# A gated cross-attention block on one core: context columns stay in order, work moves to VectorE, and two queues load the context

## The chip, the cores and the metric

The kernel runs on one core of a Trainium2 chip. The metric is the device time of one execution in microseconds; several runs are timed and the median is taken. One further execution is recorded by the hardware profiler.

## What is computed

Eight sequences of 100 rows (width 2048) attend to 722 context vectors each, in float32; then a linear layer with unpacked 6-bit weights follows.

```python
x = x + tanh(g_xattn[0]) * xattn(layernorm(x), ctx)      # x (8,100,2048), ctx (8,722,2048)
x = x + tanh(g_ffn[0]) * ffn(layernorm(x), qweight, scale, zero, bias)
# xattn: a = q @ k^T ; e = softmax(a) ; c = e @ k         (keys are also the values)
# ffn:   w = (unpack6(qweight) - zero) * scale ; x @ w^T + bias     (2048 x 2048)
```

## The kernel before

Every engine runs a list of instructions written out by hand, and semaphores tie the lists together. There is no scheduler: an engine that waits holds up all that stands behind it in its list, and SyncE's transfers are such a list too.

**Layout.** The context of batch `b` lies in `raw[:, b % 2]`, so there are two buffers and the loads for batch b overwrite batch b-2. It has 6 tiles (`NT`) of up to 128 keys. A tile is loaded in four pieces, one for each quarter of the 2048 columns (`g`, 512 columns each), and quarter g goes to partitions 32g to 32g+31. Tiles 0 to 2 are the first half of the keys and 3 to 5 the second. For the value product the same data is cut into 12 units of up to 64 keys (`UNITS`; unit u lies in tile u/2).

**Stages.** While batches last, TensorE goes round this loop for i = 0 to 6: `scores(i + 1)` (queries times keys, with the transposes of batch i's probabilities, `probs`, in between), then `attend(i)` (probabilities times values, with the transposes of batch i+2's queries, `queries`, in between). In this text a stage of batch i starts where `attend(i)` starts, and A is that moment. VectorE takes the row maximum of the scores at the same time.

- `keys_turned` (VectorE, `rT<-raw`, line 930): 16 transposes per batch, each over 12 blocks of 32x32 for two column groups, 768 columns wide. Eight belong to the first half of the keys and eight to the second. A ring of five (`RING`) lets five of the next batch be done during `attend`. Their input is read as `(k j c)`: neighbouring elements of a block lie 16 floats apart.
- `context_hi` (ScalarE, line 583) rounds a unit to float32r into one of five slots of `vhi`; `context_lo` (GpSimd, line 526) subtracts that from the unit and writes the rest to `vlo`. TensorE needs both. A tile may be overwritten when its units' low parts are made (`lo_made`) and its keys turned (`s_keys`). The transfers of the next batch but one wait for this (`used`).
- `probs`, `probs_lo`, `copy_probs`: the transposed probabilities are split in two parts and then copied by ScalarE (line 621, ten copies of 1200 columns: `MOVES`, shifts c = 1, 2, 3) to the other partition quarters.
- `ln1_norm` (ScalarE, line 587) normalizes the next queries in `xa`, 2048 columns at once, and `queries` transposes them with a column step of 16. `ln1_stats` (VectorE, line 753) takes their statistics in four pieces between the transposes of the second half. `residual` (VectorE, line 805) adds the attention result, `ln2_norm` (ScalarE, line 597) normalizes that for the linear layer, `x1_out` and `rows_out` (SyncE, lines 352 and 357) store both.

**SyncE's list** for batch b: `next_x(b)`, `x1_out(b-3)`, `rows_out(b-4)` (waits for `ln2_norm`), tiles 0 to 2 (line 328), `next_xres`, tiles 3 to 5.

**After the loop** come `attend(7)` with its preparations (`unpack` of the weights on VectorE, lines 858 to 865, and `copy_last_probs`, line 828, 20 copies of 600 columns), and then the linear layer, line 1158.

## Time and profile before

| | us |
|---|---|
| timed runs, median of 3 (lowest to highest) | 668.67 (666.34 to 671.26) |
| the profiled execution, own time | 658.23 |
| span of the profile, first to last instruction | 656.4 |
| TensorE busy | 553.9 |
| VectorE busy | 423.8 |
| ScalarE busy | 283.0 |
| GpSimd busy | 258.6 |
| mean granted TensorE clock, share of full | 0.937 |

The sum of a prediction is made against 658.23, the profiled execution's own time, and carried over to the median by its ratio. An engine's busy time says how much it does, not whether anything waits for it; the timeline and the chain of waits say that.

### The profile page before, as it was taken

To read this page: it belongs to the slowest core of one execution; us is meant where nothing else is said; L and a number is where in the kernel's file an instruction comes from. 1 tells how busy PE (TensorE), PEld (TensorE's weight loads), DVE (VectorE), ACT (ScalarE), POOL (GpSimd) and SP (SyncE) were. 2 spreads that over 40 slices of the span, in tenths; PEclk is the share of its full clock that TensorE was granted. 3 is DMA by queue.
4 is the path that set the end of the run, shared out by engine and by line. 5 is a ranking of instruction groups with operands and counts; after the bars stand their busy time and mean duration, and the time that the engine had idled before them with its cause. 6 is when DMAs were issued, how large, how long until landed. Compare 5 with 4: busy or idle time off the path is not lost.

```text
span 656.4 us, 10122 instructions
## 1 busy us (share of the span) xinstructions
PE 553.9 (84%) x4134; PEld 320.1 (49%) x4134; DVE 423.8 (65%) x538; ACT 283.0 (43%) x308; POOL 258.6 (39%) x245
## 2 busy tenths in 40 slices
PE   5746999999986897997997683296999999999997
PEld 5523565475553463463463352165565444444445
DVE  4649747949818918928917638959476856763544
ACT  1301755776863774675674542365342322120000
POOL 2008049389396197198197056657100000000000
PEclk8769899999999999899999596689899999999999
DMA  8999729847398498498499432447784599993321
GB/s 192 208 243 222 185 74 225 215 120 216 89 220 214 129 211 214 135 228 209 139 219 209 157 116 83 182 155 226 260 275 113 154 186 186 237 221 76 84 69 36
DMA packets 58376, 113.77 MB, mean 173 GB/s; under 512 B 21967, under 2 KB 22223, under 8 KB 54047
## 3 DMA queue, kind: packets, MB, share of 16 engines
q1 hardware_dynamic: 41580, 108.13, 63.1%
q10 hardware_dynamic: 16750, 5.01, 6.7%
q8 instruction: 32, 0.52, 0.3%
q14 instruction: 14, 0.11, 0.1%
HBM read 89.26 MB, written 19.66 MB: 166 GB/s over the span
## 4 chain that ended last, share of the span: by engine, by line
PE 35%; DVE 23%; DMA 17%; POOL 12%; ACT 5%; SPq 4%; issue 4%; DVEq 0%; ACTq 0%
PE S L1158 16%; DVE rT L930 11%; POOL vlo L526 11%; DMA xa<-in_x 9%; PE pv L1158 7%; PE S L1067 5%; DMA raw<-in_ctx 5%; DMA raw<-in_L_ffn_qweight 3%; DVE stats L753 3%; SPq L328 3%; DVE ph L828 2%; PE T L1036 2%; DVE raw L858 2%; PE pv L1098 1%; DVE xres L805 1%
## 5 line engine op out<-in xcount | busy, mean ns | idle before, releaser
L930 DVE STREAM_TRANSPOSE rT<-raw 128x768 f32<-128x768 f32 x129 | 183.6, 1471 | 110.8 <-DMA raw<-in_ctx 108.1
L526 POOL TENSOR_TENSOR vlo<-raw,vhi 128x1024 fp32r<-128x1024 f32 x96 | 218.4, 2313 | 28.1 <-ACT vhi L583 28.1
L1067 PE MATMUL S<-rT,qT 128*100 128x338 f32 (+3 forms) x544 | 187.2, 491 | 48.3 <-DVE rT L930 46.8
L1067 PEld LDWEIGHTS S<-rT,qT 128*100 128x100 f32 x544 | 90.8, 182 | 134.4 <-DVE rT L930 77.0
L1098 PE MATMUL pv<-vhi,ph 32*100 32x512 f32 (+1 forms) x736 | 127.7, 402 | 9.3 <-POOL vlo L526 9.3
L1098 PE MATMUL S<-vhi,ph 32*100 32x512 f32 (+1 forms) x736 | 128.1, 402 | 0.0
L583 ACT ACTIVATE vhi<-raw 128x1024 fp32r<-128x1024 f32 x96 | 94.7, 1018 | 33.3 <-PE S L1098 29.1
L621 ACT ACTIVATE ph<-ph 32x1200 fp32r<-32x1200 f32 (+1 forms) x70 | 84.1, 1202 | 36.6 <-DVE ph L819 35.0
L1098 PEld LDWEIGHTS pv<-vhi,ph 32*100 32x100 f32 (+1 forms) x736 | 62.7, 161 | 34.0 <-POOL vlo L526 15.6
L1158 PE MATMUL S<-raw 128*128 128x512 f16 x320 | 73.8, 387 | 5.1 <-issue 5.1
L1098 PE MATMUL S<-vlo,ph 32*100 32x512 f32 (+1 forms) x368 | 74.4, 392 | 0.0
L1098 PE MATMUL pv<-vlo,ph 32*100 32x512 f32 (+1 forms) x368 | 73.8, 392 | 0.0
L506 POOL TENSOR_SCALAR ln<-mr 100x1 f32<-100x1 f32 x16 | 4.2, 261 | 176.3 <-DVE mr L761 175.8
L1098 PEld LDWEIGHTS S<-vhi,ph 32*100 32x100 f32 (+1 forms) x736 | 63.4, 161 | 5.3
L1158 PEld LDWEIGHTS S<-raw 128*128 128x128 f16 x320 | 31.4, 99 | 42.6 <-ACT raw L565 5.3
L1158 PE MATMUL pv<-raw 128*128 128x512 f16 x192 | 42.6, 379 | 0.0
L1036 PE MATMUL T<-ident,xa 100*128 100x100 f32 (+2 forms) x176 | 26.2, 296 | 15.2 <-DVE ph L819 9.5
L650 ACT ACTIVATE xa<-raw 128x2048 f16<-128x2048 f16 x8 | 15.3, 1910 | 51.9 <-DVE raw L865 46.6
L908 DVE TENSOR_TENSOR late<-S,consts 128x512 f32<-128x512 f32 (+2 forms) x19 | 12.8, 673 | 34.0 <-PE S L1158 34.0
L1036 PEld LDWEIGHTS T<-ident,xa 100*128 100x128 f32 (+2 forms) x176 | 22.9, 207 | 22.6 <-issue 16.1
L1098 PEld LDWEIGHTS pv<-vlo,ph 32*100 32x100 f32 (+1 forms) x368 | 31.5, 162 | 4.3
L565 ACT ACTIVATE qT<-T 128x400 f32<-128x400 f32 x28 | 12.9, 499 | 47.3 <-PE T L1036 47.3
(107 smaller groups left out, 577.4 us busy)
## 6 DMA issues: line engine op xcount, KB each, us to landing
raw<-in_ctx SPq DMA_DIRECT2D x160, 256.0 KB, 8.9
raw<-in_L_ffn_qweight SPq DMA_DIRECT2D x16, 768.0 KB, 8.1
rows_scratch<-xres SPq DMA_DIRECT2D x8, 800.4 KB
xres<-in_x SPq DMA_DIRECT2D x8, 800.0 KB
x_scratch<-xres SPq DMA_DIRECT2D x8, 800.0 KB
late<-x_scratch SPq DMA_DIRECT2D x24, 256.0 KB, 6.6
out_y<-late SPq DMA_DIRECT2D x23, 256.0 KB, 3.8
xa<-in_x SPq DMA_DIRECT2D x6, 800.0 KB
```

What stands on the lines that cost most here:

```text
L328: sp.dma_start(tile_at(b, t)[32 * g:32 * g + 32, 0:whole * W].rearrange("i (k e) -> i k e", k=whole), ctx_in[b, first:last, g * W:(g + 1) ...
L526: pool.tensor_tensor(vlo[:, k, 0:n], keys, vhi[:, k, 0:n].bitcast(F32), ALU.subtract).then_inc(s_vlo, 1)
L583: act.activation(vhi[:, k, 0:n], keys, ACT.Copy).then_inc(s_vhi, 1)
L621: act.activation(ph[dst:dst + n, c], ph[src:src + n, 0].bitcast(F32), ACT.Copy).then_inc(s_copied, 1)
L650: act.activation(wn[n % 2], unp[n % 2].rearrange("p j g -> p (j g)").bitcast(F16), ACT.Copy, bias=-float(BIAS16)).then_inc(s_wn, 1)
L753: dve.bn_stats(stats[0:R, k, c, :], src[0:R, c * 512:(c + 1) * 512]).then_inc(s_stat[k], 1)
L828: dve.tensor_copy(ph[dst:dst + n, c, :, tiles, :], ph[src:src + n, 0, :, tiles, :].bitcast(F32)).then_inc(s_copied_last, 1)
L930: dve.transpose(rT[:, step % RING, 0:n * blocks * 32], keys[:, c:c + n]).then_inc(s_keys, 1)
L1036: last = pe.transpose(dst(T[k]), src, ident[0:n, 0:n])
L1067: last = pe.matmul(into[0:R, g, begin:begin + width], qT[:, c + e, :], rT[:, step % RING, e * blocks * 32:e * blocks * 32 + width], start= ...
L1098: last = pe.matmul(pv[g][0:R, :], probabilities(g, block, p), v[32 * g:32 * g + r, k, h * W:(h + 1) * W], start=(block == 0 and a == 0), s ...
L1158: last = pe.matmul(ACC[(j + k) % NA][0:r, cols], xT[m][:, h, c, :], WT[nb % 2][:, c, cols], start=(c == 0 and h == 0), stop=(c == CH - 1 a ...
```

## The change

Six things are edited together.

1. The keys are read for the transposes as `(k c j)`, 32 neighbouring floats at a time. The queries are put in the same column order: `centred` writes batches 0 and 1 in that order to `xres`, and `ln1_norm` becomes four operations of 512 columns into a new buffer `xq`, each waiting until TensorE has transposed the one before it. `queries` is spread over blocks 3, 6, 9 and 12 of `attend` instead of two at 11 and two at 15.
2. `load_ctx` now has an issuing engine. SyncE issues quarters 0 and 2 and ScalarE quarters 1 and 3 of every tile. ScalarE's issues stand at fixed places in its list.
3. VectorE takes the four copies with shift c = 3 from ScalarE (after transpose 8).
4. VectorE takes `context_lo` of unit 8 from GpSimd, ahead of the next batch's five transposes.
5. SyncE issues tiles 0 and 1 ahead of `rows_out`, and `next_x` waits for the normalization, not the transposes.
6. `unpack(1)` moves behind the copies of the last batch's probabilities.

```diff
+    ON_VECTOR = {8}
...
+            xq = attention.enter_context(nc.sbuf_tensor("xq", [P, 512], F32))
...
-            eng.wait_ge(s_vlo, b * UNITS + u + 1)
+            by = int(u in ON_VECTOR)
+            same = [v for v in range(UNITS) if (v in ON_VECTOR) == (u in ON_VECTOR)]
+            eng.wait_ge(s_vlo[by], b * len(same) + same.index(u) + 1)
...
+        def load_ctx(eng, quarters, b, t):
+            if b >= 2:
+                for u in (2 * t, 2 * t + 1):
+                    lo_made(eng, b - 2, u)
+                eng.wait_ge(s_keys, BASE[b - 2] + (FIRST_HALF[b - 2] if t < HALF else len(STEPS[b - 2])))
...
+            for g in quarters:
+                eng.dma_start(tile_at(b, t)[32 * g:32 * g + 32, 0:whole * W].rearrange("i (k e) -> i k e", k=whole),
+                              ctx_in[b, first:last, g * W:(g + 1) * W].rearrange("(k i) e -> i k e", i=32)).then_inc(s_raw[b % 2][t], 16)
+            if whole < 4:
+                for g in quarters:
+                    eng.dma_start(tile_at(b, t)[32 * g:32 * g + REST, whole * W:(whole + 1) * W],
+                                  ctx_in[b, last:last + REST, g * W:(g + 1) * W]).then_inc(s_raw[b % 2][t], 16)
...
-                k, u = bank("q", b - 1, 3)
-                sp.wait_ge(s_turned[k], u + 1)
+                sp.wait_ge(s_q, b * NCH)
...
             for b in range(2, B):
                 if b >= 3:
                     next_x(b)
                     x1_out(b - 3)
-                if b >= 4:
-                    rows_out(b - 4)
                 for t in range(HALF):
-                    used(b - 2, t)
-                    load_ctx(b, t)
+                    load_ctx(sp, (0, 2), b, t)
+                    if b >= 4 and t == 1:
+                        rows_out(b - 4)
...
                     next_xres(b - 2)
                 for t in range(HALF, NT):
-                    used(b - 2, t)
-                    load_ctx(b, t)
+                    load_ctx(sp, (0, 2), b, t)
...
-            def ln1_norm(b):
+            def ln1_norm(b, f):
                 act.wait_ge(s_rstd[0], b + 1)
-                act.activation(xa[0:R, 0:D], xa[0:R, 0:D], ACT.Identity, bias=shift[0:R, 0:1], scale=mr[0:R, 0, 1:2]).then_inc(s_q, 1)
+                k, u = bank("q", b - (f == 0), (f - 1) % 4)
+                act.wait_ge(s_turned[k], u + 1)
+                columns = xa[0:R, 0:D].rearrange("r (g c j) -> r c g j", g=Q, j=32)[:, 4 * f:4 * f + 4]
+                act.activation(xq[0:R, :].rearrange("r (c g j) -> r c g j", g=Q, j=32), columns, ACT.Identity,
+                               bias=shift[0:R, 0:1], scale=mr[0:R, 0, 1:2]).then_inc(s_q, 1)
...
                 for c, dst, n, src in MOVES:
-                    act.activation(ph[dst:dst + n, c], ph[src:src + n, 0].bitcast(F32), ACT.Copy).then_inc(s_copied, 1)
+                    if c < 3:
+                        act.activation(ph[dst:dst + n, c], ph[src:src + n, 0].bitcast(F32), ACT.Copy).then_inc(s_copied[0], 1)
...
+            for t in range(NT):
+                load_ctx(act, (1, 3), 0, t)
...
             contexts_hi(0, range(SLOTS))
+            for t in range(HALF):
+                load_ctx(act, (1, 3), 1, t)
...
+            for t in range(HALF, NT):
+                load_ctx(act, (1, 3), 1, t)
...
                 exps(i + 1)
+                if i + 2 < B:
+                    ln1_norm(i + 2, 0)
+                    for t in range(2):
+                        load_ctx(act, (1, 3), i + 2, t)
                 context_hi(i, 5)
                 if i + 2 < B:
-                    ln1_norm(i + 2)
-                    contexts_hi(i, range(6, 10))
-                    queries(i + 2, (0, 1))
-                    contexts_hi(i, range(10, UNITS))
-                    queries(i + 2, (2, 3))
-                    contexts_hi(i + 1, range(SLOTS))
+                    for f, units in enumerate(((6,), (7, 8), (9,), (10, 11))):
+                        if f < 3:
+                            ln1_norm(i + 2, f + 1)
+                        queries(i + 2, (f,))
+                        contexts_hi(i, units)
+                        if f in (1, 3):
+                            load_ctx(act, (1, 3), i + 2, 2 + f // 2)
+                    for u in range(SLOTS):
+                        context_hi(i + 1, u)
+                        if u in (1, 4):
+                            load_ctx(act, (1, 3), i + 2, 4 + u // 4)
...
             def centred(b):
                 dve.wait_ge(s_aggr[0], b + 1)
-                for p in [xa[0:R, c * 512:(c + 1) * 512] for c in range(NCH)] if b == 0 else [xa[0:R, 0:D]]:
-                    dve.tensor_scalar(p, p, mr[0:R, 0, 0:1], None, ALU.subtract).then_inc(s_q, 1)
+                turned = xres[b][0:R, 0:D].rearrange("r (c g j) -> r g c j", g=Q, j=32)
+                for g in range(Q):
+                    dve.tensor_scalar(turned[:, g], xa[0:R, g * W:(g + 1) * W].rearrange("r (c j) -> r c j", j=32),
+                                      mr[0:R, 0, 0:1], None, ALU.subtract).then_inc(s_q, 1)
...
+            def copy_probs(b):
+                for f in range(PF):
+                    k, u = bank("P", b, f)
+                    dve.wait_ge(s_free[k], u + 1)
+                for c, dst, n, src in MOVES:
+                    if c == 3:
+                        dve.tensor_copy(ph[dst:dst + n, c], ph[src:src + n, 0].bitcast(F32)).then_inc(s_copied[1], 1)
...
+            def context_lo(b, u):
+                k, n, keys = unit_at(b, u)
+                dve.wait_ge(s_vhi, b * UNITS + u + 1)
+                dve.tensor_tensor(vlo[:, k, 0:n], keys, vhi[:, k, 0:n].bitcast(F32), ALU.subtract).then_inc(s_vlo[1], 1)
...
-                    keys = raw[:, b % 2, first // (4 * HALF), at:at + blocks * W].rearrange("p (k j c) -> p c k j", j=32, c=CH)
+                    keys = raw[:, b % 2, first // (4 * HALF), at:at + blocks * W].rearrange("p (k c j) -> p c k j", j=32, c=CH)
                     dve.transpose(rT[:, step % RING, 0:n * blocks * 32], keys[:, c:c + n]).then_inc(s_keys, 1)
...
+                hooks = {5 + f: lambda f=f: probs_lo(i, f) for f in range(PF)} | {8: lambda: copy_probs(i)}
...
                 coef(i + 1)
+                for u in sorted(ON_VECTOR):
+                    context_lo(i, u)
                 if i + 2 < B:
                     keys_turned(i + 2, range(RING))
-            unpack(1)
             probs_lo(LAST, 0)
             rows_lo(0, 0)
             copy_last_probs(0)
             residual(LAST - 1)
             probs_lo(LAST, 1)
             copy_last_probs(1)
+            unpack(1)
...
-                    pe.wait_ge(s_q, b + NCH)
-                    turn("q", b, f, [(at(j, R), xa[0:R, 4 * f + j:D:CH], R) for j in range(4)])
+                    pe.wait_ge(s_q, b * NCH + (f + 1 if b >= 2 else NCH))
+                    at_x = xres[b][0:R, 4 * f * P:4 * (f + 1) * P] if b < 2 else xq[0:R, :]
+                    turn("q", b, f, [(at(j, R), at_x[:, j * P:(j + 1) * P], R) for j in range(4)])
...
-                            pe.wait_ge(s_copied, len(MOVES) * (b + 1))
+                            for k, copies in enumerate(((1, 2), (3,))):
+                                pe.wait_ge(s_copied[k], sum(c in copies for c, *_ in MOVES) * (b + 1))
...
                 if i + 2 < B:
-                    attend(i, {11: lambda: queries(i + 2, (0, 1)), 15: lambda: queries(i + 2, (2, 3))})
+                    attend(i, {3 + 3 * f: lambda f=f: queries(i + 2, (f,)) for f in range(4)})
```

How the lists change, at three places. VectorE, from the row maximum of one stage into the next; before (`rT<-raw` are the key transposes, `stats` the statistics, `ph<-T,ph` is `probs_lo`):

```order
L784 TENSOR_REDUCE soft<-S 100x1
...
L797 TENSOR_SCALAR soft<-soft,tg 100x1
L930 STREAM_TRANSPOSE rT<-raw 128x768 x5
...
L819 TENSOR_TENSOR ph<-T,ph 128x300
L930 STREAM_TRANSPOSE rT<-raw 128x768 x3
L753 BN_STATS stats<-xa 100x6
```

and now:

```order
L820 TENSOR_REDUCE soft<-S 100x1
...
L833 TENSOR_SCALAR soft<-soft,tg 100x1
L879 TENSOR_TENSOR vlo<-raw,vhi 128x1024
L981 STREAM_TRANSPOSE rT<-raw 128x768 x5
...
L855 TENSOR_TENSOR ph<-T,ph 128x300
L981 STREAM_TRANSPOSE rT<-raw 128x768 x2
L865 CAST ph<-ph 32x1200 x4
L981 STREAM_TRANSPOSE rT<-raw 128x768
L787 BN_STATS stats<-xa 100x6
```

The low part of unit 8 stands ahead of the five early transposes, and four copies stand between transposes 8 and 9 (counted from 0).

ScalarE during `attend`, before (`vhi<-raw` is `context_hi`, `qT<-T` the copies of the queries):

```order
L607 ACTIVATE E,soft<-S,soft 100x722
L583 ACTIVATE vhi<-raw 128x1024
L587 ACTIVATE xa<-xa,shift,mr 100x2048
L583 ACTIVATE vhi<-raw 128x1024 x4
L565 ACTIVATE qT<-T 128x400 x2
```

and now:

```order
L624 ACTIVATE E,soft<-S,soft 100x722
L603 ACTIVATE xq<-xa,shift,mr 100x512
L340 DMA raw<-in_ctx 32x4x512 x4
L596 ACTIVATE vhi<-raw 128x1024
L603 ACTIVATE xq<-xa,shift,mr 100x512
L578 ACTIVATE qT<-T 128x400
L596 ACTIVATE vhi<-raw 128x1024
L603 ACTIVATE xq<-xa,shift,mr 100x512
L578 ACTIVATE qT<-T 128x400
L596 ACTIVATE vhi<-raw 128x1024 x2
L340 DMA raw<-in_ctx 32x4x512 x2
```

Four issues now stand ahead of unit 5, two behind unit 8, and eight more follow further on in the stage.

SyncE, one batch; before:

```order
L343 DMA xa<-in_x 100x2048
L352 DMA x_scratch<-xres 100x2048
L357 DMA rows_scratch<-xres 100x2049
L328 DMA raw<-in_ctx 32x4x512 x12
L348 DMA xres<-in_x 100x2048
```

and now:

```order
L357 DMA xa<-in_x 100x2048
L369 DMA x_scratch<-xres 100x2048
L340 DMA raw<-in_ctx 32x4x512 x4
L374 DMA rows_scratch<-xres 100x2049
L340 DMA raw<-in_ctx 32x4x512 x2
L365 DMA xres<-in_x 100x2048
```

SyncE's halves of tiles 0 and 1 have moved ahead of the store that waits for `ln2_norm`.

## Rows read from the trace of the kernel before

**Rows 1.** The page's chain that ended last, by line.

```profile
PE S L1158 16%; DVE rT L930 11%; POOL vlo L526 11%; DMA xa<-in_x 9%; PE pv L1158 7%; PE S L1067 5%; DMA raw<-in_ctx 5%; DMA raw<-in_L_ffn_qweight 3%; DVE stats L753 3%; SPq L328 3%; DVE ph L828 2%; PE T L1036 2%; DVE raw L858 2%; PE pv L1098 1%; DVE xres L805 1%
```

**Rows 2.** Windows by stage: busy per engine, clock, DMA share, GB/s.

```profile
89.30:132.20 42.90, 40.64 (x366) 24.37 (x369) 29.86 (x31) 29.20 (x31) 29.15 (x21) 1.00 0.71 178
...
174.40:226.10 51.70, 42.00 (x367) 24.36 (x370) 32.01 (x36) 31.33 (x33) 31.13 (x29) 1.00 0.77 190
...
276.10:324.60 48.50, 42.88 (x366) 24.55 (x366) 32.26 (x35) 31.33 (x33) 31.09 (x29) 0.96 0.78 190
324.60:380.80 56.20, 45.03 (x367) 26.79 (x370) 31.38 (x36) 31.33 (x33) 30.77 (x27) 0.88 0.82 196
380.80:459.00 78.20, 47.17 (x654) 34.32 (x654) 58.56 (x71) 35.56 (x43) 51.08 (x38) 0.84 0.43 150
```

**Rows 3.** VectorE groups by shape: total us, mean ns, idle before.

```profile
L930 DVE STREAM_TRANSPOSE rT<-raw 128x768 f32<-128x768 f32 x127 | 182.1, 1482 | 110.8 <-DMA raw<-in_ctx 108.1 <-PE S L1067 2.6
...
L784 DVE TENSOR_REDUCE soft<-S 100x1 f32<-100x722 f32 x6 | 5.5, 909 | 4.5 <-PE S L1067 4.5
...
L930 DVE STREAM_TRANSPOSE rT<-raw 128x512 f32<-128x512 f32 x1 | 1.0, 1021 | 0.0
```

**Rows 4.** Waits of SyncE's queue: total us, times, longest.

```profile
SPq L357 <- ACT xres L597: 94.8, 7, 17.8
SPq L328 <- POOL vlo L526: 94.7, 25, 21.3
```

**Rows 5.** Timeline of SyncE's issues, 250 to 300 us: start, length.

```profile
271.83 0.28 SPq L357 DMA_DIRECT2D rows_scratch<-xres  x1
272.22 11.10 SPq L328 DMA_DIRECT2D raw<-in_ctx  x12
...
298.38 0.32 SPq L343 DMA_DIRECT2D xa<-in_x  x1
```

**Rows 6.** Windows inside the stage from 276.1, columns as in rows 2.

```profile
272.20:313.10 40.90, 35.85 (x344) 21.33 (x343) 24.64 (x29) 24.06 (x27) 31.11 (x28) 0.97 0.91 217
313.10:320.50 7.40, 6.83 (x20) 3.10 (x19) 7.40 (x8) 7.27 (x7) 0.00 (x0) 0.91 0.12 49
```

**Rows 7.** Timeline of VectorE in that stage: start, length, idle before.

```profile
292.67 7.12 DVE L930 STREAM_TRANSPOSE rT<-raw 128x768 f32<-128x768 f32 x5 [12.69 <-DMA raw<-in_ctx]
...
309.95 2.84 DVE L930 STREAM_TRANSPOSE rT<-raw 128x768 f32<-128x768 f32 x2 [2.59 <-DMA raw<-in_ctx]
313.08 0.69 DVE L753 BATCH_NORM_STATS2 stats<-xa 100x6 f32<-100x512 f32 x1 [0.28 <-DMA xa<-in_x]
...
324.65 0.91 DVE L784 TENSOR_REDUCE soft<-S 100x1 f32<-100x722 f32 x1 [0.60 <-PE S L1067]
```

**Rows 8.** Timeline of GpSimd in the stage from 276.1.

```profile
282.05 13.06 POOL L526 TENSOR_TENSOR vlo<-raw,vhi 128x1024 fp32r<-128x1024 f32 x6 [0.49 <-ACT vhi L583]
...
297.73 11.65 POOL L526 TENSOR_TENSOR vlo<-raw,vhi 128x1024 fp32r<-128x1024 f32 x5
```

**Rows 9.** Timeline of VectorE in the stage from 89.3.

```profile
110.33 1.43 DVE L805 SCALAR_TENSOR_TENSOR xres<-pv,soft,xres 100x512 f32<-100x512 f32 x2
```

**Rows 10.** VectorE's copies of line 828: shortest, median, longest ns.

```profile
L828 DVE CAST ph<-ph x20: 460/466/2576, 410.2 to 431.0; 32x600 fp32r<-32x600 f32 x16, 64x600 fp32r<-64x600 f32 x4
```

**Rows 11.** Timeline of VectorE, 380 to 430 us.

```profile
393.60 8.98 DVE L858 TENSOR_SCALAR raw<-raw 128x512 uint16<-128x512 uint16 x1 [8.96 <-DMA raw<-in_L_ffn_qweight]
...
410.19 13.14 DVE L828 CAST ph<-ph 32x600 fp32r<-32x600 f32 x10
```

**Rows 12.** Timeline of GpSimd over the same time.

```profile
386.99 15.24 POOL L526 TENSOR_TENSOR vlo<-raw,vhi 128x1024 fp32r<-128x1024 f32 x7
...
412.54 9.97 POOL L526 TENSOR_TENSOR vlo<-raw,vhi 128x1024 fp32r<-128x1024 f32 x4 [7.58 <-ACT vhi L583]
```

**Rows 13.** ScalarE's one plain issue of a transfer, ns.

```profile
L679 ACTq DMA_DIRECT2D xa<-in_x x1: 602/602/602, 60.0 to 60.0; - x1
```

**Rows 14.** SyncE's issues of whole blocks of context, ns.

```profile
L328 SPq DMA_DIRECT2D raw<-in_ctx x192: 311/432/4863, 2.3 to 344.9; - x192
```

56 lines of the change are left out of this document (27 added, 29 removed).

## The prediction, written before the changed kernel ran

> **What bounds the kernel now.** I read the chain of waits first. Three kinds of work share it: TensorE in the linear layer, VectorE's key transposes (11%) and GpSimd's low parts (11%), with transfers between them [rows 1]. So no single engine is full all the time, and the stages have to be read one by one. The windows by stage [rows 2] show what differs. A stage lasts 42.9 us at 89.3 (the next one 42.2), but then 51.7, 50.0, 48.5 and 56.2. All engines are busy for about the same time in each; what grows is idle time. VectorE's transposes waited 108.1 us in all for context to land [rows 3]: the long stages are late on data.
>
> Why the data is late is in SyncE's own waits: 94.8 us in 7 waits for ScalarE's `ln2_norm` ahead of `rows_out`, up to 17.8 us each [rows 4]. The store goes out at 271.83 and the first context piece of the stage right behind it at 272.22 [rows 5], although room had been there for long. From 272.2 to 313.1 the DMA engines are 91% busy; in the 7.4 us behind that, 12% [rows 6]. VectorE shows both ends: with A = 276.1, the first half is in at 292.67 (A+16.6), the second at 309.95 (A+33.8), the queries' rows at 313.08 (A+37.0), and the row maximum of the next stage stands at 324.65, 14.7 us after the second half came [rows 7]. GpSimd makes the low parts back to back from 282.05 to 295.1, and those of the next batch from 297.73 to 309.4, A+33.3 [rows 8]. In the short stages nothing is late: `residual` starts at 110.33, A+21.0 [rows 9], and VectorE works through to the end.
>
> **The change, part by part.**
>
> *Transposes.* One of 768 columns takes 1482 ns, one of 512 takes 1021 [rows 3]: 1.80 ns a column with neighbours 16 floats apart. No transpose of neighbouring elements is in the trace. The nearest row of VectorE with neighbouring float32 elements is the row maximum, 722 columns in 909 ns [rows 3], so 0.97 us for 768. The bounds are 0.97 and 1.48. I take 0.97 since 1.80 ns a column is far from what the row maximum does per column, and the step is what differs in kind. In a row, five take 7.12 us [rows 7], 1.42 each, 0.06 less than one alone; so 0.9 each after, 0.5 saved on each of 16. Of these, five are covered by `attend` in either kernel; eleven, 5.5 us, can stand on the path, and in a data-bound stage only the eight behind the second half, 4.2 us.
>
> The Trainium skill ("SBUF — State Buffer", Door 1: The DMA port swizzle) says that consecutive accesses within a 16-byte line run at full rate and each step to a new line pays. By it the change removes the penalty wholly. This trace shows only the strided form.
>
> *Copies.* VectorE now makes four of 1200 columns. The shortest of its copies of 600 took 0.46 us [rows 10]; with another 600 at the same rate, 0.8 us. But the ten at 410.19 took 13.14 us [rows 11] while GpSimd made four low parts of 2.5 us each [rows 12], and the longest copy took 2.58 [rows 10]. So four cost 3.1 to 3.2 us with GpSimd idle and up to 10 with it busy. ScalarE saves four of 1.2 us, which is not on the path; it lets `ln2_norm` and `rows_out` come some 4 us earlier.
>
> *Low part of unit 8.* GpSimd saves about 2.2 us (13.06 us for five long ones and a short one [rows 8]). VectorE pays at the row maximum's rate 1024/722 x 0.91 = 1.3 us, and covers it before the data is in. Whether it gets in between GpSimd's operations is the question of the first rival.
>
> *Issues by ScalarE.* 14 per stage. The one plain issue by ScalarE in the trace took 602 ns [rows 13]; SyncE's took 0.43 at the median and 4.86 at worst [rows 14], with 12 in 11.10 us when many stand in the queue [rows 5]. So 0.43 to 0.93 each, 6 to 13 us per stage; I take 0.6, since ScalarE's queue holds few at a time: 8.4 us against 4.8 us of copies saved, on an engine that is busy for 31.3 of 48.5 us. Of these, four stand ahead of unit 5 (2.4 us, with 1.5 us given back by the smaller normalization) and two behind unit 8. With 12 units in 21 us, TensorE comes to unit 5 near A+8.7; GpSimd was through with it before 282.05, A+5.9 [rows 8], so some 2.8 us of cover stand against 0.9 more; units 9 to 11 come one behind the other, and `attend` ends at A+21, as now. Their wait for unit 8 and its tile holds up what stands behind: ScalarE's halves of tiles 4 and 5 can't go before the slots of units 8 and 11 are free, near A+18 and A+22.
>
> *Landing.* In the stage at 276.1, 40.9 us at 217 GB/s move about 8.9 MB [rows 6]. What now goes out before A is `rows_out` (0.8 MB) and SyncE's halves of tiles 0 and 1 (four of 256 KB, 1.05 MB); it uses the idle time. What stays between A+3 and the landing of the second half and the queries' rows is 5.9 MB of context less 1.05, and two loads of 0.8 MB: 6.4 MB, 29.6 us at 217 GB/s. So the second half lands near A+33, with the rows, against A+33.8 and A+37.0. That is only 0.8 us better for the keys since the halves by ScalarE start late.
>
> *The path after it.* From A+33, VectorE: one transpose 0.9, four copies 3.1 (GpSimd is through at A+33.3), then 0.9 and a piece of statistics 0.6, three times (two transposes 1.8 and one piece 0.6), and from the last piece to the row maximum 0.9: 13.6 us. The next stage starts at A+46.6. The same count for the kernel before gives 2.84 from 309.95, a wait of 0.3, 0.6 + 3 x 3.4 and 0.9, 324.8; the row says 324.65.
>
> *Short stages.* From A+21: `residual` 2.8, four transposes 3.6, `probs_lo` twice 0.9, so A+28.3; the copies then meet GpSimd's low parts of the next batch until A+33.3, and end near A+36.4; 9.6 more give A+46. **These stages get slower by 3 us each.** All stages then take 46 to 47.
>
> *Sum.* First row maximum of the loop at 89.3: eight faster transposes behind the queries' rows but a little more queued ahead of them, -3. Then 46 + 46 + 3 x 46.6, and 48 for the last one of the loop, where the first weights are waited for (now 56.2): 279.8 against 380.8 - 89.3 = 291.5, -11.7. After the loop, `unpack(1)` waited 9.0 us for its weights, then needed 8.98 us for its first piece, the other four followed, and only then came the copies [rows 11]. Behind them now, the copies start about 10 us earlier, but meet GpSimd's low parts again: -9, and TensorE takes this up since it stands idle there (47 us busy in 78.2 [rows 2]). The linear layer is unchanged. Together -24: from 658.23 to 634.5, by the ratio 0.964 on the median **644 us**. 1% is about what a measurement of this kernel can tell from no change.
>
> **The rivals.**
>
> *VectorE doesn't get in at unit 8 (slower).* At 393.60 one VectorE operation on 512 columns took 8.98 us [rows 11] while GpSimd ran seven low parts without a gap, from 386.99 to 402.2 [rows 12]: it was let in only when that row ended. Where the trace shows this, the Trainium skill ("SBUF — State Buffer", Who interferes with whom) has the rule: a VectorE operation with two SBUF inputs and a GpSimd one that reads SBUF exclude each other for the whole instruction. The low part of unit 8 would wait in the same way until unit 11 is made, A+19. TensorE would then have units 8 to 11 before it, 5.5 us, and end `attend` at A+26; slots, tiles and landing shift by the same, and a stage takes 51.6. Six stages cost +18 against now, the two `attend` behind the loop +10; with -3 and -9 that is +16, **685 us** on the median. It decides from there being no gap in GpSimd's row between units 7 and 9. Against it: ScalarE has two issues, a normalization and a query copy between units 8 and 9, some 2.8 us, so that GpSimd should wait about 1 us there. Chance 0.12.
>
> *The transposes stay at 1.4 us.* Then the path behind the landing is 4 us longer, stages take 50.8, and all but the tail is given back: about +3, **671 us**. Chance 0.12.
>
> *The issues are slow.* With 0.93 us each, units 9 to 11 come 2 us late and the second half lands near A+36: stages of 49.6, -6, **662 us**. Chance 0.13.
>
> *The copies slip in and two queues move more.* Copies done by A+32 in all stages and the second half in at A+30: 43.5 a stage, another -18, **625 us**. For it: the queue is at 190 GB/s over a stage but 217 in the busy part [rows 2, 6]. Against it: the rule (same skill, "DMA: Bandwidth & Descriptors", Issuing engines are not separate DMA queues) that a second issuing engine saves issue time alone; the trace has no stretch with two full queues. Chance 0.18.
>
> **How the numbers follow.** My forecast has 0.45. The range of 80% reaches from just under the fast case, 622, to 674, past the strided one; the case at unit 8 is left out. Faster by over 1% (below 662): 0.45 and 0.18, half of the slow-issue case and a little of the rest, 0.71. Within 1%: the rest of that and most of the transposes' case, 0.14. Slower: 0.15.
>
> **What would show it.** Right: transposes of 768 columns near 0.97 us; stages all between 45 and 48, with the first two longer than now; `rows_out` no longer ahead of a row of context; copies of 0.8 us behind the landing and of 2 us or more in the short stages; the first copy behind the loop near 400. Wrong: a long unit 8 on VectorE with TensorE waiting for it; ScalarE issues over 0.9 us; landing after A+35; or an early part in which ScalarE's context pieces hold up the first rows of x so long that the first scores start late.

## The result, and the profile after it

The changed kernel takes 697.56 us, median of 4 runs (689.58 to 700.25); the kernel before took 667.5 beside it (659.37 to 671.26). The ratio is 1.045, 95% interval 1.028 to 1.062: **slower, by 30 us, where 24 us faster was forecast.** The profiled execution took 689.58, its span is 687.2 (before 656.4). Ratios here and below are of each kernel's fast runs alone (none over 1.5% above its fastest, e9 has one), while medians and spreads are of all runs, and the profiles of e2, e6, e9 and e11 are of slower ones.

The windows by stage of the changed kernel, columns as in [rows 2], cut at the row maxima:

```profile
95.43:143.93 48.50, 42.08 (x366) 24.71 (x370) 28.05 (x37) 25.27 (x30) 27.49 (x19) 0.93 0.65 157
143.93:191.06 47.13, 41.64 (x366) 24.92 (x370) 30.22 (x40) 27.39 (x32) 30.23 (x30) 0.93 0.69 179
191.06:242.56 51.50, 42.79 (x366) 25.02 (x370) 30.23 (x40) 27.17 (x32) 29.41 (x27) 0.90 0.76 180
242.56:295.93 53.37, 44.04 (x366) 25.71 (x370) 30.32 (x41) 27.17 (x32) 30.04 (x29) 0.87 0.73 173
295.93:344.80 48.87, 42.39 (x366) 24.76 (x370) 30.23 (x40) 27.29 (x32) 28.34 (x21) 0.93 0.80 189
344.80:398.35 53.55, 43.99 (x366) 25.65 (x370) 29.57 (x41) 27.01 (x32) 29.05 (x26) 0.87 0.81 187
398.35:489.50 91.15, 53.41 (x655) 37.52 (x656) 67.47 (x75) 36.55 (x43) 47.62 (x36) 0.77 0.37 130
489.50:687.20 197.70, 191.00 (x1080) 95.44 (x1080) 114.47 (x196) 36.66 (x40) 3.47 (x12) 0.99 0.70 157
```

The whole loss can be placed with them. Up to the first row maximum: 95.43 against 89.3, +6.1. The six stages: 302.9 against 291.5, +11.4. From the last row maximum to the linear layer's first product: 91.15 against 78.9, +12.2. The linear layer: +1.0. The sum, 30.7, is the difference of the spans (30.8) but for rounding. The forecast for the same four was -3, -11.7, -9 and 0.

VectorE by shape, columns as in [rows 3]:

```profile
L981 DVE STREAM_TRANSPOSE rT<-raw 128x768 f32<-128x768 f32 x127 | 116.6, 952 | 98.9 <-DMA raw<-in_ctx 94.1 <-PE S L1123 4.6
L879 DVE TENSOR_TENSOR vlo<-raw,vhi 128x1024 fp32r<-128x1024 f32 x8 | 33.8, 4221 | 46.3 <-ACT vhi L596 46.3
L865 DVE CAST ph<-ph 32x1200 fp32r<-32x1200 f32 x28 | 21.7, 776 | 0.9
L820 DVE TENSOR_REDUCE soft<-S 100x1 f32<-100x722 f32 x6 | 5.5, 909 | 15.3 <-PE S L1123 15.3
```

A transpose fell from 1482 to 952 ns, as forecast; 65 us of VectorE work are gone. Waiting for context is still 94 us. The sizes of the transposes and the copies were right, so the loss lies elsewhere: in what waits for what. The first full stage shows it (VectorE's timeline: start, length, idle before):

```profile
120.69 0.96 DVE L981 STREAM_TRANSPOSE rT<-raw 128x768 f32<-128x768 f32 x1
128.99 0.98 DVE L981 STREAM_TRANSPOSE rT<-raw 128x768 f32<-128x768 f32 x1 [7.35 <-DMA raw<-in_ctx]
130.00 3.20 DVE L865 CAST ph<-ph 32x1200 fp32r<-32x1200 f32 x4
133.23 0.98 DVE L981 STREAM_TRANSPOSE rT<-raw 128x768 f32<-128x768 f32 x1
...
143.93 0.91 DVE L820 TENSOR_REDUCE soft<-S 100x1 f32<-100x722 f32 x1 [1.91 <-PE S L1123]
```

With A = 95.4: VectorE is idle for 7.35 us until the second half lands at A+33.6. In the kernel before no such wait stood in this stage; its three transposes around that point ran in one row:

```profile
116.43 4.33 DVE L930 STREAM_TRANSPOSE rT<-raw 128x768 f32<-128x768 f32 x3
```

In the changed kernel then come one transpose, the four copies (3.20 us) and the rest; and the row maximum waits another 1.9 us for TensorE. Why TensorE is late, narrower windows of the same stretch tell, columns as in [rows 2]:

```profile
122.00:130.00 8.00, 4.45 (x14) 2.00 (x12) 0.98 (x2) 6.06 (x6) 3.91 (x2) 1.00 0.81 220
...
132.00:134.20 2.20, 0.31 (x1) 0.00 (x0) 2.14 (x4) 0.00 (x0) 0.00 (x0) 0.50 0.48 121
134.20:136.00 1.80, 1.74 (x3) 0.99 (x4) 1.80 (x4) 0.00 (x0) 0.00 (x0) 0.50 0.01 2
136.00:138.00 2.00, 2.00 (x6) 1.08 (x5) 2.00 (x4) 0.00 (x0) 0.00 (x0) 0.71 0.00 0
138.00:140.00 2.00, 2.00 (x8) 1.17 (x7) 2.00 (x3) 0.00 (x0) 0.00 (x0) 1.00 0.00 0
```

TensorE had little to do while the landing was waited for (4.45 of 8 us), and during the copies nearly nothing (0.31 of 2.2). Its granted clock then stands at 0.50, which is 1.2 GHz, until about 137, and at 2.4 GHz from 138. A transposed block is four matmul records. The trace has their starts 0.57 us apart until 137.2 and 0.28 us apart from there, so 2.3 us a block at half clock and 1.1 at the full one; VectorE, with a piece of statistics behind every second transpose, needs about 1.2. Just behind a late landing TensorE is the slower of the two.

### The profile page after: what moved, and what is told of

Its sections match the earlier page's. It is cut to its first block, busy times and chain, and to the rows that moved or that the text cites. A ratio compares the mean times of both kernels' runs of the same rounds, so it can differ in the third digit from the quotient of the medians.

```text
span 687.2 us, 10212 instructions
## 1 busy us (share of the span) xinstructions
PE 563.7 (82%) x4134; PEld 325.3 (47%) x4134; DVE 407.8 (59%) x577; ACT 253.7 (37%) x298; POOL 246.1 (36%) x237
## 4 chain that ended last, share of the span: by engine, by line
PE 39%; DMA 25%; DVE 15%; POOL 9%; issue 4%; ACT 4%; ACTq 2%; SPq 1%; DVEq 0%
DMA raw<-in_ctx 19%; PE S L1215 14%; PE S L1123 12%; POOL vlo L538 8%; PE pv L1215 7%; DVE ph L865 3%; DVE rT L981 3%; DVE ph L873 2%; DMA raw<-xa 2%; ACTq L340 2%; PE pv L1155 2%; DVE vlo L879 2%; DMA xa<-rows_scratch 2%; PE T L1091 2%; ACT vhi L596 2%
## 5 line engine op out<-in xcount | busy, mean ns | idle before, releaser
L1123 PE MATMUL S<-rT,qT 128*100 128x338 f32 (+3 forms) x544 | 192.0, 512 | 60.7 <-DVE rT L981 59.4
L538 POOL TENSOR_TENSOR vlo<-raw,vhi 128x1024 fp32r<-128x1024 f32 (+1 forms) x88 | 205.6, 2370 | 61.0 <-ACT vhi L596 60.9
L981 DVE STREAM_TRANSPOSE rT<-raw 128x768 f32<-128x768 f32 x129 | 117.5, 946 | 98.9 <-DMA raw<-in_ctx 94.1
L1123 PEld LDWEIGHTS S<-rT,qT 128*100 128x100 f32 x544 | 99.3, 194 | 142.5 <-DVE rT L981 67.9
L1155 PE MATMUL pv<-vhi,ph 32*100 32x512 f32 (+1 forms) x736 | 131.9, 414 | 9.1 <-DVE vlo L879 5.3
L1155 PE MATMUL S<-vhi,ph 32*100 32x512 f32 (+1 forms) x736 | 131.7, 413 | 0.0
L879 DVE TENSOR_TENSOR vlo<-raw,vhi 128x1024 fp32r<-128x1024 f32 x8 | 33.8, 4221 | 46.3 <-ACT vhi L596 46.3
L639 ACT ACTIVATE ph<-ph 32x1200 fp32r<-32x1200 f32 (+1 forms) x42 | 50.5, 1202 | 18.3 <-DVE ph L855 17.5
L1215 PEld LDWEIGHTS S<-raw 128*128 128x128 f16 x320 | 31.3, 99 | 42.3 <-ACT raw L578 5.2
L624 ACT ACTIVATE E<-S,soft 100x722 f32<-100x722 f32 x6 | 5.2, 866 | 87.8 <-DVE soft L820 87.8
L668 ACT ACTIVATE xa<-raw 128x2048 f16<-128x2048 f16 x8 | 15.3, 1910 | 55.8 <-DVE raw L916 46.0
L1155 PEld LDWEIGHTS S<-vlo,ph 32*100 32x100 f32 (+1 forms) x368 | 32.1, 168 | 1.6
## 6 DMA issues: line engine op xcount, KB each, us to landing
raw<-in_ctx SPq DMA_DIRECT2D x80, 256.0 KB, 11.7
```

The costliest lines, as they stand in the source:

```text
L538: pool.tensor_tensor(vlo[:, k, 0:n], keys, vhi[:, k, 0:n].bitcast(F32), ALU.subtract).then_inc(s_vlo[0], 1)
L639: act.activation(ph[dst:dst + n, c], ph[src:src + n, 0].bitcast(F32), ACT.Copy).then_inc(s_copied[0], 1)
L668: act.activation(wn[n % 2], unp[n % 2].rearrange("p j g -> p (j g)").bitcast(F16), ACT.Copy, bias=-float(BIAS16)).then_inc(s_wn, 1)
L879: dve.tensor_tensor(vlo[:, k, 0:n], keys, vhi[:, k, 0:n].bitcast(F32), ALU.subtract).then_inc(s_vlo[1], 1)
L981: dve.transpose(rT[:, step % RING, 0:n * blocks * 32], keys[:, c:c + n]).then_inc(s_keys, 1)
L1123: last = pe.matmul(into[0:R, g, begin:begin + width], qT[:, c + e, :], rT[:, step % RING, e * blocks * 32:e * blocks * 32 + width], start= ...
```

## The experiments

Each edit of the change was undone alone in the changed kernel, then all four of the disputed ones together, then three of them were put back one at a time. "Stages" is the sum of the six, "first" the first row maximum of the loop, "tail" the stretch behind it up to the linear layer, all from the profiled execution.

| kernel | median us (lowest to highest, runs) | ratio to before (95%) | first | stages | tail |
|---|---|---|---|---|---|
| before | 667.5 (659.37 to 671.26, 4) | 1 | 89.3 | 291.5 | 78.9 |
| changed | 697.56 (689.58 to 700.25, 4) | 1.045 (1.028 to 1.062) | 95.4 | 302.9 | 91.1 |
| e1: copies undone | 674.66 (670.27 to 679.09, 4) | 1.017 (1.008 to 1.025) | 93.4 | 282.2 | 91.2 |
| e2: `unpack(1)` undone | 684.5 (674.7 to 688.48, 4) | 1.024 (1.011 to 1.036) | 97.1 | 310.0 | 79.0 |
| e3: unit 8 undone | 705.46 (694.0 to 711.65, 4) | 1.053 (1.040 to 1.067) | 96.9 | 311.5 | 90.2 |
| e4: split undone | 673.44 (670.49 to 677.84, 4) | 1.015 (1.007 to 1.024) | 89.6 | 290.0 | 91.0 |
| e5: all four undone | 641.61 (639.68 to 651.26, 6) | 0.970 (0.961 to 0.980) | 84.4 | 279.6 | 78.8 |
| e9: e5 and unit 8 | 648.14 (634.66 to 652.75, 4) | no interval | 82.2 | 271.7 | 78.6 |
| e10: e5 and copies | 660.63 (651.51 to 667.33, 4) | 0.987 (0.973 to 1.001) | 85.6 | 289.1 | 78.2 |
| e11: as e10, copies earlier | 663.65 (653.49 to 670.61, 10) | 0.993 (0.986 to 0.999) | 82.6 | 291.6 | 78.8 |
| e12: e5 and split | 666.65 (656.17 to 677.11, 10) | 1.000 (0.992 to 1.008) | 94.2 | 285.7 | 79.0 |

The kernel before, run beside each group, had medians of 665.67 (e1 to e4), 670.59 (e5 to e8) and 666.15 (e9 to e12), and spread over 657 to 681 us, so two single profiles can differ by over 3% with nothing changed. The columns "first", "stages" and "tail" are of one profile each, and a difference of a few us in them proves nothing by itself.

**e1, the copies back on ScalarE.**

```diff
                 for c, dst, n, src in MOVES:
-                    if c < 3:
-                        act.activation(...).then_inc(s_copied[0], 1)
+                    act.activation(...).then_inc(s_copied[0], 1)
-hooks = {5 + f: ... probs_lo ...} | {8: lambda: copy_probs(i)}
+hooks = {5 + f: ... probs_lo ...}
```

TensorE's wait for the copies is changed to match.

> The changed kernel, with the four copies of shift c = 3 back on ScalarE. Theory P (TensorE paces the scores at about 1.38 us for each transposed block, so that any VectorE work of 3.2 us between transposes 8 and 9 lies on the path): the gap of VectorE behind transpose 8 closes, each of the six stages gets about 3 us shorter, and the span falls from 687 by 17 to 20 us. Rival L (the landing of context sets the stage, copies are hidden beside it): under 5 us in all, the stages keep 48 to 53 us.

23 us faster than the changed kernel, 20.7 of it in the six stages: 3.45 us each, where the copies took 3.20. That is what theory P said of the stages. The span fell by 11.5 us only, not by 17 to 20: in the linear layer of this profile TensorE waited 10.2 us once for weights.

**e2, `unpack(1)` back to where it was.**

```diff
+            unpack(1)
             probs_lo(LAST, 0)
...
             copy_last_probs(1)
-            unpack(1)
```

> The changed kernel, with the second weight tile unpacked ahead of the last batch's copies again. Theory Q (the move holds up SyncE's list: the load of the fourth weight tile waits for that unpacking, and the load of normalized rows stands behind it): SyncE's wait for VectorE's unpacking falls from 43 to under 20 us, the linear layer starts some 8 to 12 us earlier counted from the start of the seventh attention, and the six stages are unchanged; span 675 to 679. Rival (the part behind the loop is late through VectorE being held by GpSimd): no gain or a loss of up to 5 us, since the copies start later again.

The tail is 79.0 us, 12.1 shorter, and the run 13 us faster, as theory Q said. Its stages are 7 us longer in this profile, which this edit doesn't explain. SyncE's list in the changed kernel (start, length of the row of issues) shows who was held up:

```profile
406.99 44.45 SPq L408 DMA_DIRECT2D raw<-in_L_ffn_qweight  x3
...
453.19 0.38 SPq L422 DMA_DIRECT2D xa<-rows_scratch  x1
```

The third of these weight loads needs the buffer that `unpack(1)` reads. With `unpack(1)` behind the copies, it and everything queued behind it on SyncE wait: the constants, the rows for the linear layer, the store of the last rows. In SyncE's waits, for the changed kernel and then for e2:

```profile
SPq L408 <- DVE raw L916: 54.9, 4, 43.3
```

```profile
SPq L408 <- DVE raw L916: 26.3, 4, 14.9
```

And VectorE's timeline shows that the copies gained little by going first:

```profile
405.19 13.35 DVE L879 TENSOR_TENSOR vlo<-raw,vhi 128x1024 fp32r<-128x1024 f32 x1 [2.99 <-ACT vhi L596]
...
423.51 13.14 DVE L873 CAST ph<-ph 32x600 fp32r<-32x600 f32 x10
```

They start 25.2 us after the row maximum (before 29.4 [rows 11]), so 4.2 us sooner and not 10; the place that `unpack(1)` left was taken by unit 8, held for 13.35 us.

**e3, unit 8 back on GpSimd.**

```diff
-    ON_VECTOR = {8}
+    ON_VECTOR = set()
```

> The changed kernel, with the low part of unit 8 back on GpSimd. Theory: in the stages VectorE's operation of 3.2 us costs TensorE nothing (no wait in the trace), but in the seventh attention it was held 13.4 us and TensorE waited about 5.5 us; so the span falls by 4 to 7 us. Rival (GpSimd is the tighter one, and the relief shortens each attention): the span grows by 1 to 2 us a stage, 6 to 12 us.

Not faster: 705.46 against 697.56, with overlapping spreads, and the stages of this profile are 8.6 us longer. That is the side of the rival, but not clear of noise. The held subtraction is real, but taking it away brought nothing, not even in the tail (90.2): there SyncE's queue decided.

**e4, all context pieces issued by SyncE.**

```diff
-load_ctx(sp, (0, 2), b, t)          # and the same for batches 0 and 1
+load_ctx(sp, (0, 2, 1, 3), b, t)
-load_ctx(act, (1, 3), ...)          # all six places
```

> The changed kernel, with all four quarters issued by SyncE and none by ScalarE; the order of tiles and stores stays. Theory S (ScalarE's halves of tiles 0, 1 and 5 start late since they stand behind its other work): in the first two full stages the second half lands 5 us or more earlier, and they fall from 48.5 and 47.2 to about 44; later stages gain 0 to 3 us each; span 665 to 677. Rival (the rate of the DMA engines alone sets the landing): landings stay at A+32 to A+37 and the span within 5 us of 687.

24 us faster. The first row maximum comes at 89.6 instead of 95.4 and the first full stage takes 44.1 instead of 48.5. The second takes 47.5, not the 44 of theory S: its data is in early, and the copies then meet GpSimd and take 7.8 us. ScalarE's timeline of the changed kernel shows what left late:

```profile
61.38 3.84 ACTq L340 DMA_DIRECT2D raw<-in_ctx  x6
...
97.22 0.34 ACTq L340 DMA_DIRECT2D raw<-in_ctx  x1
...
116.50 0.74 ACTq L344 DMA_DIRECT2D raw<-in_ctx  x2
```

Half of tiles 3 to 5 of batch 1 leaves only from 61.38 on, behind the queries; in e4 SyncE has sent all of them by 53.3. In the first full stage ScalarE's halves of tiles 0 and 1 leave at A+1.8 to A+3.1, behind the exponentials, where in e4 both tiles were in by A-1.5. A half tile is no use, so in these two places the later half sets the landing.

For the last tile of the stage this is not so. ScalarE's pieces of it leave by A+21.8, which is no later than e4 sends its last ones. SyncE's lists in the two kernels, first the changed kernel's (A = 95.4), then e4's (A = 89.6):

```profile
115.30 0.71 SPq L344 DMA_DIRECT2D raw<-in_ctx  x2
116.05 0.31 SPq L357 DMA_DIRECT2D xa<-in_x  x1
```

```profile
110.51 1.42 SPq L344 DMA_DIRECT2D raw<-in_ctx  x4
```

In e4 the last piece leaves by A+22.3 and the tile is in at A+26.9; in the changed kernel it leaves by A+21.8 and is in at A+33.4. What differs is the company. SyncE, rid of half of its issues, sends the rows of x at A+20.6, while ScalarE's pieces are still on their way. The two DMA queues from 119 to 128.83 show it (packets, MB, share of the 16 engines):

```profile
q1 hardware_dynamic: 409, 1.76, 78.4%
q10 hardware_dynamic: 183, 0.27, 13.2%
```

q10 is ScalarE's queue: over the whole run it moved 28.7 MB, against 5.0 in e5, where ScalarE issues no context. In these 9.8 us it got 27 GB/s, for the rest of a tile that everything waits for, and SyncE's q1 got 179 for rows of x, a store and the next pieces of context, none of which anything waits for yet. The split alone is shown as the cause (here and by e12); how much of it is the company and how much the late halves of tiles 0 and 1, no run separates.

**e5, all four undone.** What stays: the transposes of neighbours with `xq` and the four `ln1_norm`, and SyncE's new order. The edits of e1 to e4 together.

> The changed kernel with the copies on ScalarE, the second unpacking early, unit 8 on GpSimd and all loads by SyncE: what is left is the column order with its faster transposes, the normalization in four parts, and SyncE's order of tiles and stores. Theory P (TensorE needs about 1.38 us for each transposed block, so that a transpose of 0.9 us gains next to nothing): the span is at most 10 us below that of before, 646 to 656, and what is gained comes from the order of loads; VectorE stands idle for TensorE. Rival (the faster transposes do count once nothing is put in their way): 8 to 11 transposes a stage save 4 to 5 us, 25 us or more in all, a span near 630.

641.61 us, 0.970 of before: **this part of the change is a gain of 3%, some 20 us, and the four others together lose 50 us by the ratios, 56 by the medians.** The span, 640.4, lies between the two theories. VectorE's timeline of its first stage shows what is gone, the wait for the second half (the transposes run on in one row), and what is late next, the queries' rows:

```profile
110.29 2.91 DVE L968 STREAM_TRANSPOSE rT<-raw 128x768 f32<-128x768 f32 x3
116.45 0.69 DVE L774 BATCH_NORM_STATS2 stats<-xa 100x6 f32<-100x512 f32 x1 [3.25 <-DMA xa<-in_x]
...
125.25 0.91 DVE L807 TENSOR_REDUCE soft<-S 100x1 f32<-100x722 f32 x1 [0.88 <-PE S L1110]
```

**e6, only SyncE's order, in the kernel before.**

```diff
-                if b >= 4:
-                    rows_out(b - 4)
                 for t in range(HALF):
                     used(b - 2, t)
                     load_ctx(b, t)
+                    if b >= 4 and t == 1:
+                        rows_out(b - 4)
```

> The kernel before with one edit: SyncE issues tiles 0 and 1 ahead of the store of normalized rows. Theory: the four long stages wait less for their first half, but VectorE's path of 14.7 us behind the landing stays; 2 to 4 us a stage, span 642 to 650. Rival (the DMA engines' rate sets the landing, the order doesn't): within 4 us of 656. Against the kernel with columns reordered, this tells what the faster transposes are worth: nothing if the two are within 5 us.

667.13 us (12 runs), ratio 0.994, 0.987 to 1.001: nothing that can be told from zero, which is the rival's side. In its profile the first half of the keys is in some 4 to 8 us sooner in the four long stages, at A+12.2 to A+13.0, but the second half only at A+31.5 to A+34.4, and the six stages take 289.8 us. So most of e5's gain belongs to the transposes with what goes with them: the four parts of `ln1_norm`, the queries spread over `attend`, and `next_x` waiting for less. These were not taken apart, nor was the order tried with fast transposes only.

**e7 and e8, half of TensorE's score work, in the kernel before and in e5.** Both leave out the products of the odd column groups but the last, so nearly half of the score products are missing.

```diff
                     for e in range(n):
+                        if (c + e) % 2 and c + e != CH - 1:
+                            continue
```

> The kernel before with nearly half of the score products left out (odd column groups but the last are skipped, so the output is of other scores); all transposes stay. Theory P says VectorE at 1.42 us and TensorE at 1.38 us a block are level in the kernel before, so taking half of TensorE's work there shortens a stage by under 1 us, span 648 to 656.

> The kernel with the column order alone, with the same products left out. Theory P: now TensorE was the slower one, so the stages get shorter by 3 to 5 us each against the same kernel with all products, 20 to 35 us in all. Rival (landing or VectorE sets the pace): under 8 us in all.

One run each: 661.9 for e7, 632.22 for e8 (spans 660.1 and 630.4). The kernel before gained nothing that shows (its stages took 297.1 us); e5 gained 10 us, 7.6 of them in the six stages (272.0 against 279.6), which is the side of the rival. TensorE's pace seems to matter only once the transposes are fast, and then by 1.3 us a stage, not by the 20 us or more expected in all. It is a weak test: with half of the products gone the mean granted clock fell too, to 0.857 in e7 and 0.884 in e8 (0.937 and 0.938 with all of them), so what was left ran slower.

**e9, e5 with unit 8 on VectorE.** In e5, `ON_VECTOR = {8}`.

> The columns kernel (642 us, six stages 280 us together) with one more edit: the rest of unit 8 is made by VectorE. Theory H (VectorE's subtraction is held while GpSimd's run, 13.35 us once and 3.2 us in most stages of the changed kernel, but nothing waits for it there): within 3 us of the columns kernel, 639 to 645. Rival W (the held subtraction delays the next stage's transposes one for one): six stages longer by 6 to 20 us, 648 to 662. Rival G (GpSimd's list is one subtraction shorter, raw tiles come free 1.3 us earlier per stage): 634 to 638.

The profile is better up to the linear layer, which starts 10.2 us earlier (stages 271.7 against 279.6): the side of the third theory. Then its TensorE waits 12.1 us for weights, and the total is lost in the spread (634.66 to 652.75; the best of its four runs is faster than each of e5's six). In e9 the subtraction takes 2.6 us in a stage and is not held for long. With e3 this makes two bases on which the stages are about 8 us shorter when VectorE makes unit 8, one profile each: perhaps a gain, not shown.

**e10, e5 with the copies on VectorE.** The edit of e1 turned round, in e5.

> The columns kernel with one more edit: VectorE makes the third set of copies behind transpose 8, as in the changed kernel. Theory P (the copies lie between the landing of the second half and the transposes that wait for it, 3.2 us each without a wait and more beside GpSimd's subtractions): six stages longer by 16 to 25 us, about 660 us. Rival S (TensorE paces what follows the landing, and VectorE catches the copies up): six stages longer by under 6 us, 641 to 648. Rival C (ScalarE is rid of its copies and issues its later work earlier, which pays for it): under 640.

19 us slower than e5 by the medians, 1.7% of before (11 us) by the ratios, and 9.5 us in the stages of this profile, which is of the fastest of its four runs. That is more than rival S has and less than theory P. VectorE's timeline of the copies in the first three of the six stages (the other three also took 3.20 us):

```profile
113.35 6.49 DVE L853 CAST ph<-ph 32x1200 fp32r<-32x1200 f32 x4
156.92 9.12 DVE L853 CAST ph<-ph 32x1200 fp32r<-32x1200 f32 x4
211.47 3.20 DVE L853 CAST ph<-ph 32x1200 fp32r<-32x1200 f32 x4
```

3.2 us behind a late landing, with GpSimd done; 6.5 and 9.1 where the data is early and GpSimd is at work. Both sizes stand in the prediction.

**e11, the copies ahead of the wait.**

```diff
-{8: lambda: copy_probs(i)}
+{7: lambda: copy_probs(i)}
```

> As the run before, but the copies stand behind transpose 7, ahead of the wait for the second half instead of behind it. Theory P, if the place is what costs: where VectorE waits for the landing anyhow (up to 6 us in the columns kernel) they are free, so the stages are within 6 us of the columns kernel's 280, 636 to 648 us, and 10 to 20 us faster than the run with the copies behind transpose 8. Rival R (the writes to ph or the shared port with GpSimd cost, wherever they stand): as slow as that run, about 660.

The theory of the place fell: no faster than e10 (ratio 0.993 against 0.987). The copies were to fill VectorE's wait for the second half, but there GpSimd makes its low parts:

```profile
155.22 10.00 DVE L853 CAST ph<-ph 32x1200 fp32r<-32x1200 f32 x4
205.39 9.58 DVE L853 CAST ph<-ph 32x1200 fp32r<-32x1200 f32 x4
```

In the six stages they took 7.3, 10.0, 9.6, 9.3, 8.7 and 9.9 us, three times the length without GpSimd. Neither place is good.

**e12, e5 with the split.** The edit of e4 turned round, in e5.

> The columns kernel with one more edit: ScalarE issues the second and fourth column quarter of every tile. Theory Q (ScalarE's halves stand behind exponentials, tile 5 until 20 us into a stage, and in batch 1 behind the queries): first full stage starts 5 to 8 us later, the six stages take 5 to 15 us more, 650 to 665 us. Rival N (the transfers are bound by how much moves, not by who issues; the loss seen before came from the split together with the copies): within 3 us, 639 to 645. Rival T (two queues move more than one): landing earlier and 5 us or more faster, under 636.

25 us slower than e5 by the medians, 2.9% of before (19 us) by the ratios, and back at the time of the kernel before. The first row maximum is at 94.2 again (e5 84.4), the stages take 285.7. The second half lands later in the first stages: at A+35.1 in the first one, where e5 has no wait for it. And ScalarE's halves of tiles 0 and 1 hold up the first half: in the long stages it is in at A+20.9 to A+23.1, in e5 at A+12.9 to A+14.2.

**The parts add up.** Undone alone in the changed kernel, the four change the ratio by -2.9% (copies), -2.2% (`unpack(1)`), +0.8% (unit 8) and -3.0% (split), -7.2% together before rounding; all undone give -7.5%. Put back alone on e5, copies cost 1.7% and the split 2.9%. Each of these has an uncertainty of 1 to 2%, so the split costs the same on either base, the copies agree within the noise, and unit 8 can't be told from zero. A single profile couldn't have told any of this with this spread.

## Why the prediction was wrong, step by step

*Transposes: size right, worth less than counted.* 0.95 us each, or 0.91 in a row, against the 0.9 taken. I counted 4.2 us saved behind the landing. In the stage at 95.4 the way from there to the row maximum took 14.9 us; without the copies 11.7, against 14.7 in [rows 7]: 3.0 saved. The rest went to TensorE, which I had left out of the path: at 1.2 GHz after its idle time it needs over 2 us a block. Over the six stages the row maximum waited 15.3 us for TensorE (4.5 before [rows 3]).

*Copies: size right, cost right.* 3.20 us behind the landing were forecast and measured. The 6.5 to 10 us beside GpSimd, forecast for the short stages, did not come in the changed kernel, where the late landing put the copies behind GpSimd's work; with an early landing they came (e4, e10). The size has luck in it: 0.46 us for 600 columns makes 0.92 for 1200 at the same rate, and the 0.8 of the sum had no row. Over six stages that is 19 us, and e1 measured 20.7. The path of 13.6 us that I worked out had them in it, so they are no error of the sum. They were bought at a price that I had worked out and put up with.

*The path after the landing: TensorE left out.* It took 15.5 us in the mean of the six stages against the 13.6 of the sum, and these 1.9 us are nearly all the row maximum's wait for TensorE, 2.6 us a stage in the mean where [rows 7] have 0.6. The sum followed VectorE alone.

*Landing: the step that failed in the stages.* The forecast was A+33 in long stages and no wait in the two short ones. The first transpose of the second half starts at A+33.6, 31.5, 36.2, 36.9, 35.0 and 37.1, mean 35.0 (at 35.0 the data was in at A+34.8, and TensorE held the transpose too). That is 2.0 us over the forecast, and with the 1.9 us of the path six times 3.9 make 23 us, the whole error of the stages (302.9 against 279.8).

In the long stages the megabytes of the sum were right and the rate was not. From A+3 to that transpose, the fourth stage of the changed kernel (A = 242.6) and of the kernel before (A = 226.1), columns as in [rows 2]:

```profile
245.56:279.41 33.85, 27.72 (x294) 16.97 (x292) 14.48 (x19) 24.75 (x28) 27.74 (x19) 0.97 0.92 193
```

```profile
229.09:261.59 32.50, 27.88 (x282) 16.91 (x274) 15.40 (x18) 19.29 (x22) 29.17 (x20) 1.00 0.93 212
```

193 to 204 GB/s in the four of them, with 6.5 to 6.8 MB moved, where I took 6.4 MB at 217; before it was 212 to 216. Why the rate is lower is open: e4 and e5, without the split, have 180 to 187 there, with less to move. In the short stages I had no landing in the sum at all. There the queues moved this from A = 95.4 until the tile was in, in the changed kernel and then in e5 from A = 84.4 to A+26.7:

```profile
q1 hardware_dynamic: 1469, 3.65, 46.8%
q10 hardware_dynamic: 1654, 2.96, 37.7%
```

```profile
q1 hardware_dynamic: 2215, 4.24, 65.2%
```

6.6 MB against 4.2, from halves of tiles 0 and 1 that were no longer in ahead of the stage, and from rows that SyncE now sent beside ScalarE's pieces instead of behind them. That the split is the cause is shown: with it alone (e12) the transpose starts at A+35.1, 31.3, 38.4, 36.1, 36.0 and 37.5, and without it (e5) in the four long stages at A+32.8, 32.9, 31.2 and 35.4, in the short ones without a wait. I had seen that ScalarE's halves of tiles 4 and 5 would go out late (near A+18 and A+22), and they did, but SyncE's go out no sooner. What I had not asked is what SyncE sends in the meantime.

*Issue cost: taken too high.* ScalarE's issues of whole blocks took 0.45 us at the median, against 0.6 taken:

```profile
L340 ACTq DMA_DIRECT2D raw<-in_ctx x96: 317/453/1747, 0.7 to 365.4; - x96
```

So the third rival, slow issues, is out as a mechanism, though the late landing it was to cause came true in another way.

*First row maximum: -3 forecast, +6.1 measured.* The split again, by the place of its issues; the prediction had named it at its end as what would make it wrong, for the rows of x, and it came by tiles 3 to 5 of batch 1. e4 takes it away, e12 brings it back.

*Tail: -9 forecast, +12.2 measured.* "The copies start about 10 us earlier" failed (4.2 us), and I had not asked what is queued on SyncE behind the weight load that waits for `unpack(1)`. e2 shows this by itself.

*Unit 8.* The held subtraction of the first rival happened, once, behind the loop's last row maximum: 13.35 us from 405.19, until a row of six on GpSimd was over:

```profile
404.53 12.92 POOL L538 TENSOR_TENSOR vlo<-raw,vhi 128x1024 fp32r<-128x1024 f32 x6
```

In the stages it took 3.2 us. The Trainium skill ("SBUF — State Buffer", Who interferes with whom) has the two engines exclude each other for a whole instruction; the trace agrees that they exclude each other, and shows more: here VectorE was held over a row of GpSimd's instructions, not one. The price of the rival (16 us more than before) isn't what was lost: e3 took unit 8 back and gained nothing.

*The fourth rival, two queues moving more.* From 105 to 130 us in the first stage 220 to 233 GB/s moved, where [rows 6] have 217 in a full stretch. That is little more, in the long stages it was less (193 to 204), and no stage came near the 43.5 us of this rival. The Trainium skill ("DMA: Bandwidth & Descriptors", Issuing engines are not separate DMA queues) expects no more from a second issuing engine, and the trace agrees.

What stays open: the wait of 0 to 12.1 us for transposed weights early in the linear layer (e1, e6, e9, e11, e12 have it, e5 and e10 hardly or not). No run was made on it; it hides up to 12 us of what a kernel gained before.

## What to carry to other kernels

A transfer cut in two between issuing engines lands when the later half does. Ask of each piece where it stands in its engine's list, and also what the other engine will send while the piece is on its way: what used to stand behind it in one list now goes beside it and takes its share of the rate. Make the sum of bytes for every stage, the short ones too, with all that both engines issue before the landing. Before a consumer of a buffer is moved back, read the list of the engine that refills it: everything queued behind that load moves too. When six edits go together, price each both ways, undone alone and done alone; here one edit gained 20 us, three others lost more than twice that, and one did nothing that shows.

## What the runs showed of the hardware

A VectorE transpose of 32 by 32 blocks in float32 takes 952 ns for 768 columns with neighbours read together, and 1482 with neighbours 64 bytes apart. Four VectorE copies of 1200 columns on 32 partitions, with one input each, take 3.20 us alone and up to 10.0 beside GpSimd's subtractions (e11), at both places that were tried. One VectorE subtraction of 1024 columns took 1.23 us free of GpSimd (at 458.9 in the changed kernel), 3.2 in the stages, and 13.35 when it was held over a row of six on GpSimd. Two issuing engines have a DMA queue each, and these share the rate unevenly: 27 GB/s for the last context pieces beside 179 for what SyncE had sent after them. TensorE's granted clock fell to 0.50 at 130.3, after 8 us in which it had been busy for 4.45, and the matmuls took twice as long until it rose at 137.2. So a late landing costs more than its own wait.
